# Sixteen-head attention on Trainium2: score matmuls on 32 rows of the array, over dense q and k stacks

## What is computed

```python
scores = einsum('bthd,bshd->bhts', q, k) / sqrt(8)
scores = where(causal, scores, -inf)      # third of the three stages only
attn = softmax(scores, axis=-1)
out = einsum('bhts,bshd->bthd', attn, v)
x = x + out @ Wo + bo                     # first and third stage; the second has no projection
```

## Time and profile before

| | us |
|---|---|
| median of 3 runs | 2067.69 (2063.5 to 2068.28) |
| profiled execution | 2068.89 |
| its span in the profile | 2066.9 |
| PE busy over the span | 1612.5 (78%) |
| DVE busy | 1384.6 (67%) |
| ACT busy | 944.4 (46%) |
| POOL busy | 776.1 (38%) |

### The profile page before, as it was taken

The page is one execution under the profiler, slowest core; times in us unless marked ns, Lnnn a source line. Parts: engine busy times, 40 slices in busy tenths (PEclk is TensorE's granted clock), DMA queues, the critical chain, the costliest instruction groups (busy, mean ns, idle before and its releaser), DMA issues. The chain is left out here.

```text
span 2066.9 us, 42332 instructions
## 1 busy us (share of the span) xinstructions
PE 1612.5 (78%) x14686; PEld 1273.3 (62%) x14686; DVE 1384.6 (67%) x4103; ACT 944.4 (46%) x1817; POOL 776.1 (38%) x1156
## 2 busy tenths in 40 slices
PE   5888873877799989788885899998549799999440
PEld 3666552876577778455553566665449699997330
DVE  4777754238787777577775799997547577774632
ACT  2666630533343334366663677777114344443010
POOL 2222226345300000211113677774454544442435
PEclk9999985887799999699997899999559799999555
DMA  6131301841000000000000000000038000000043
GB/s 181 49 129 69 107 6 37 251 143 41 25 1 2 0 1 1 6 9 7 8 5 1 1 2 2 2 2 1 16 113 234 22 15 13 14 14 3 21 135 89
DMA packets 60417, 91.88 MB, mean 44 GB/s; under 512 B 11588, under 2 KB 49493, under 8 KB 59669
## 3 DMA queue, kind: packets, MB, share of 16 engines
q1 hardware_dynamic: 54068, 76.67, 12.1%
q0 software_dynamic: 6144, 12.60, 2.1%
HBM read 72.71 MB, written 35.39 MB: 52 GB/s over the span
## 5 line engine op out<-in xcount | busy, mean ns | idle before, releaser
L666 DVE TENSOR_REDUCE parts<-PS 128x8 fp32r<-128x1024 f32 x192 | 234.8, 1223 | 120.5 <-PE PS L424 119.4
L862 ACT ACTIVATE P<-PS 128x1024 f32<-128x1024 f32 x192 | 197.0, 1026 | 153.6 <-PE PS L439 153.4
L840 ACT CAST qS<-PS 32x512 fp32r<-32x512 f32 x384 | 220.9, 575 | 9.1 <-PE PS L391 5.7
L272 POOL TENSOR_TENSOR ve<-mv,eps_t 128x1 f32<-128x1 f32 x160 | 33.1, 207 | 443.1 <-DVE mv L268 443.0
L1633 DVE SCALAR_TENSOR_TENSOR X<-PS,wt,X 128x128 f32 (+1 forms) x480 | 134.7, 344 | 47.3 <-PE PS L1476 39.7
L1476 PEld LDWEIGHTS PS<-w_f_w,P 128*128 128x128 f32 x1024 | 130.0, 193 | 39.2 <-issue 27.3
L1765 ACT ACTIVATE P<-PS,w_f_b 128x512 f32<-128x512 f32 x128 | 88.0, 687 | 142.2 <-PE PS L1457 140.8
L1476 PE MATMUL PS<-w_f_w,P 128*128 128x128 f32 x1024 | 142.1, 283 | 13.1 <-DVE X L1633 11.2
L439 PE MATMUL PS<-qS,kS 128*128 128x512 f32 x384 | 148.0, 440 | 1.0 <-ACT P L862 1.0
L760 POOL TENSOR_TENSOR rrs<-rsq,neg_half 128x20 f32<-128x20 f32 x32 | 114.3, 3571 | 74.2 <-DVE rsq L595 74.2
L391 PE MATMUL PS<-ident_r,parts 128*128 128x128 f32 x768 | 122.1, 292 | 23.2 <-issue 22.5
(11 more groups left out here) (300 smaller groups left out, 4283.4 us busy)
## 6 DMA issues: line engine op xcount, KB each, us to landing
tok<-hs SPq DMA_DIRECT2D x62, 128.0 KB, 3.2
hs<-yo SPq DMA_DIRECT2D x62, 128.0 KB, 3.6
P<-in_f_blob SPq DMA_DIRECT2D x12, 578.0 KB, 4.7
Y<-in_f_blob SPq DMA_DIRECT2D x11, 578.0 KB, 4.9
ctxT<-in_ctxT SPq DMA_DIRECT2D x128, 48.0 KB, 1.7
P<-in_f_blob SPq DMA_DIRECT2D x12, 450.0 KB, 4.0
Y<-in_f_blob SPq DMA_DIRECT2D x11, 450.0 KB, 4.2
w_f_w<-in_f_w SPq DMA_DIRECT2D x2, 1024.0 KB, 5.7
```

What stands on the lines that cost most here:

```text
L666: e.tensor_reduce(parts[:, it.s, 0, 8 * half:8 * half + 8, 3, 0], S_ps[:, :, :].rearrange("p i (j t) -> p (i j) t", t=T), AXX, ALU.max)\
L840: m = e.copy(qS[r, it.s % 2, :, j, :], TP[0][r, :].rearrange("p (g t) -> p g t", g=4))
L862: e.activation(P[:, it.s % 2, 8 * half:8 * half + 8, :].rearrange("p h t -> p (h t)"), ST_ps[:, :, :].rearrange("p j n -> p (j n)"), ACT.E ...
```

## The change

In the three stages the maximum is now taken from the same split stacks as the probabilities. `pe_turn`, `v_kx`/`a_kx`, `a_qT` and the block-diagonal `a_qS` are gone. `pe_stack_q` and `pe_stack_k` run at lag L, before the maximum is known; ACT copies them whole (`a_qA`, `a_kS`). `pe_scores` then makes one matmul per head: 24 array rows of `qA` (the parts without the maximum's place) against 24 rows of `kD`, 128 columns, eight matmuls a half that go in turn to two blocks of 32 array rows. When the maxima are in `parts`, `pe_stack_q_max` (lag L + 1) turns the q stack a second time and `a_qB` copies it; `pe_scoresT` (lag L + 1) makes one matmul per head on 32 rows, again eight a half. L becomes 3 or 5, while the last lag O stays 6 or 9. The three tiles `qA`, `qB`, `kD` lie in the memory of the old `qS`. The order of the steps on PE and ACT is written anew, one order for all three stages. In the masked stage POOL clears `vx` at the start; in the cross stage its clearing of `qS` is gone. The parameter `pre` is given by no caller, so `lead` is 0 and its branches are not built.

```diff
-            L = 4 if causal else 2
-            G = L + 4
-            O = L + 5 if causal else L + 4
+            L = 5 if causal else 3
+            G = L + 3
+            O = L + 4 if causal else L + 3
...
-            n_pad = 3 if kind == "cross" else 2 if masked else 0
-            s_turn, s_kx, s_qT = sem("turn"), sem("kx"), sem("qT")
-            s_tk, s_kS, s_tq, s_qS = (sem(n) for n in ("tk", "kS", "tq", "qS"))
+            n_pad = 3 if masked else 2 if kind == "cross" else 0
...
+            stacks = qS[:].rearrange("p b g j t -> p (b g j t)")
+            qA = stacks[:, 0:1024].rearrange("p (b g t) -> p b g t", b=2, g=4)
+            qB = stacks[:, 1024:2048].rearrange("p (b g t) -> p b g t", b=2, g=4)
+            kD = stacks[:, 2048:4096].rearrange("p (b g t) -> p b g t", b=RING, g=4)
...
-                before_it = it.n - (L - F) + 1
-                if due(before_it):
-                    e.wait_ge(s_kx, at(s_kx, before_it))
-                    e.wait_ge(s_qT, at(s_qT, before_it))
+                if due(it.n):
+                    e.wait_ge(s_fr, at(s_fr, it.n))
...
-            def pe_turn(e, it):
-
-                e.wait_ge(s_fr, at(s_fr, following(it, L - F)))
-                e.wait_ge(s_qkf, at(s_qkf, (2 if causal else 1) * (it.n + 1)))
-                for which in range(2):
-                    m = e.transpose(FR[:, which * T:(which + 1) * T],
-                                    qk[:, it.s % 2, which, :, :].rearrange("p h d -> p (h d)"), ident[:, :])
-                m.then_inc(s_turn, 1)
...
             def pe_stack_k(e, it):
                 e.wait_ge(s_lo, at(s_lo, 2 * it.n + 2))
-                if due(it.n - (O - L - 1)):
-                    e.wait_ge(s_added, at(s_added, it.n - (O - L - 1)))
-                if causal and due(it.n - (G - L - 1)):
-                    e.wait_ge(s_eg, at(s_eg, it.n - (G - L - 1)))
+                if due(it.n - (O - L)):
+                    e.wait_ge(s_added, at(s_added, it.n - (O - L)))
+                if causal and due(it.n - (G - L)):
+                    e.wait_ge(s_eg, at(s_eg, it.n - (G - L)))
                 if due(it.n):
                     e.wait_ge(s_kS, at(s_kS, it.n))
-                turn_stack(e, it, 1, s_tk)
+                turn_stack(e, it, 1, 1, s_tk)
 
             def pe_stack_q(e, it):
                 e.wait_ge(s_lo, at(s_lo, 2 * it.n + 2))
+                if due(it.n - 1):
+                    e.wait_ge(s_qB, at(s_qB, it.n - 1))
+                turn_stack(e, it, 0, 0, s_t1)
+
+            def pe_stack_q_max(e, it):
                 e.wait_ge(s_mx, at(s_mx, 2 * it.n + 2))
-                if due(it.n):
-                    e.wait_ge(s_qS, at(s_qS, it.n))
-                turn_stack(e, it, 0, s_tq)
+                e.wait_ge(s_qA, at(s_qA, following(it, 2)))
+                turn_stack(e, it, 0, 0, s_t2)
 
             def pe_scores(e, it, half):
                 if half == 0:
-                    e.wait_ge(s_qT, at(s_qT, it.n + 1))
-                    e.wait_ge(s_kx, at(s_kx, it.n + 1))
+                    e.wait_ge(s_kS, at(s_kS, it.n + 1))
+                    e.wait_ge(s_qA, at(s_qA, it.n + 1))
                 if due(2 * it.n + half):
                     e.wait_ge(s_mx, at(s_mx, 2 * it.n + half))
                 if causal:
                     for i in range(2):
                         e.matmul(S_ps[:, i, :], ident_r[:, :], causal_q[:, :], start=True, stop=False)
-                for i in range(2):
-                    r = 32 * (2 * half + i)
-                    m = e.matmul(S_ps[:, i, :], qT[r:r + 32, it.s, :],
-                                 kx[r:r + 32, it.s % 2, :, :].rearrange("p j t -> p (j t)"),
-                                 start=not causal, stop=True)
+                for g in range(4):
+                    for i in range(2):
+                        r = 32 * (2 * half + i)
+                        m = e.matmul(S_ps[:, i, g * T:(g + 1) * T], qA[r:r + 24, it.s % 2, g, :],
+                                     kD[r:r + 24, it.s, g, :], start=not causal, stop=not causal or g == 3)
                 m.then_inc(s_s, 1)
...
             def pe_scoresT(e, it, half):
                 if half == 0:
-                    e.wait_ge(s_kS, at(s_kS, it.n + 1))
-                    e.wait_ge(s_qS, at(s_qS, it.n + 1))
+                    e.wait_ge(s_qB, at(s_qB, it.n + 1))
                 if due(2 * it.n + half):
                     e.wait_ge(s_exp, at(s_exp, 2 * it.n + half))
-                for i in range(2):
-                    g = 2 * half + i
-                    if causal:
+                if causal:
+                    for i in range(2):
                         e.matmul(ST_ps[:, i, :], ident_r[:, :], causal_k[:, :], start=True, stop=False)
-                    m = e.matmul(ST_ps[:, i, :], kS[:, it.s % 2, g, :],
-                                 qS[:, it.s % 2, g, :, :].rearrange("p j t -> p (j t)"),
-                                 start=not causal, stop=True)
+                for g in range(4):
+                    for i in range(2):
+                        r = 32 * (2 * half + i)
+                        m = e.matmul(ST_ps[:, i, g * T:(g + 1) * T], kD[r:r + 32, it.s, g, :],
+                                     qB[r:r + 32, it.s % 2, g, :], start=not causal, stop=not causal or g == 3)
                 m.then_inc(s_st, 1)
...
-                                     P[:, it.s % 2, 4 * g + j, :], start=(j == 0), stop=(j == 3))
+                                     P[:, it.s % 2, 4 * j + g, :], start=(j == 0), stop=(j == 3))
...
+                for item in unrolled(O + lead):
+                    if it := item(L + lead):
+                        pe_stack_q(e, it)
+                        pe_stack_k(e, it)
+                    if it := item(L + 2 + lead):
+                        pe_values(e, it, 0)
+                    if it := item(L + 1 + lead):
+                        pe_stack_q_max(e, it)
+                    if it := item(L + lead):
+                        pe_scores(e, it, 0)
+                    if it := item(L + 2 + lead):
+                        pe_values(e, it, 1)
+                    if it := item(L + 1 + lead):
+                        pe_scoresT(e, it, 0)
+                    if it := item(F + lead):
+                        pe_hT(e, it)
+                    if it := item(L + lead):
+                        pe_scores(e, it, 1)
+                    if causal and (it := item(G)):
+                        pe_gate(e, it)
+                    if it := item(L + 1 + lead):
+                        pe_scoresT(e, it, 1)
+                    if it := item(F + lead):
+                        pe_qkv(e, it)
+                    if it := item(O + lead):
+                        pe_out(e, it)
...
-            def v_kx(e, it):
-                e.wait_ge(s_turn, at(s_turn, it.n + 1))
-                e.tensor_tensor(kx[:, it.s % 2, :, :], FR[:, T:2 * T].unsqueeze(1).broadcast_to([D, 4, T]),
-                                jmask[:, :].unsqueeze(2).broadcast_to([D, 4, T]), ALU.mult).then_inc(s_kx, 1)
...
-                e.tensor_reduce(parts[:, it.s, 0, 8 * half:8 * half + 8, 3, 0],
-                                S_ps[:, :, :].rearrange("p i (j t) -> p (i j) t", t=T), AXX, ALU.max)\
+                e.tensor_reduce(parts[:, it.s, 0, :, 3, 0].rearrange("p (g j) -> p j g", j=4)[:, 2 * half:2 * half + 2],
+                                S_ps[:, :, :].rearrange("p i (g t) -> p i g t", t=T), AXX, ALU.max)\
                  .then_inc(s_mx, 1)
...
+                if masked:
+                    e.memset(vx[:], 0.0).then_inc(s_pad, 1)
                 if kind == "cross":
-                    e.memset(qS[:].bitcast(F32), 0.0).then_inc(s_pad, 1)
...
             def a_kS(e, it):
+                if due(2 * (it.n - RING + 1)):
+                    e.wait_ge(s_st, at(s_st, 2 * (it.n - RING + 1)))
+                e.wait_ge(s_tk, at(s_tk, it.n + 1))
+                e.copy(kD[:, it.s].rearrange("p g t -> p (g t)"), TP[1]).then_inc(s_kS, 1)
+
+            def a_qA(e, it):
+                if due(2 * (it.n - 1)):
+                    e.wait_ge(s_s, at(s_s, 2 * (it.n - 1)))
+                e.wait_ge(s_t1, at(s_t1, it.n + 1))
+                e.copy(qA[:, it.s % 2].rearrange("p g t -> p (g t)"), TP[0]).then_inc(s_qA, 1)
+
+            def a_qB(e, it):
                 if due(2 * (it.n - 1)):
                     e.wait_ge(s_st, at(s_st, 2 * (it.n - 1)))
-                e.wait_ge(s_tk, at(s_tk, it.n + 1))
-                e.copy(kS[:, it.s % 2].rearrange("p g t -> p (g t)"), TP[1]).then_inc(s_kS, 1)
-
-            def a_qS(e, it):
-                if due(2 * (it.n - 1)):
-                    e.wait_ge(s_st, at(s_st, 2 * (it.n - 1)))
-                e.wait_ge(s_tq, at(s_tq, it.n + 1))
-                for j in range(4):
-                    r = slice(32 * j, 32 * j + 32)
-                    m = e.copy(qS[r, it.s % 2, :, j, :], TP[0][r, :].rearrange("p (g t) -> p g t", g=4))
-                m.then_inc(s_qS, 1)
...
```

(14 more changed lines are left out.)

190 lines of the change are left out of this document (53 added, 137 removed).

## The result

The changed kernel took 2542.96 us (median of 4 runs, 2526.4 to 2556.19), the kernel before 2067.53: a ratio of 1.230, 95% interval 1.227 to 1.233. It is slower, as predicted, but by 475 us and not by 90, far outside the range of 2085 to 2235. The profiled execution took 2526.4 us with a span of 2524.6.

What follows compares the result with a forecast made beforehand. It took a chain over several engines, closed by ACT, to bound the cross stage, and full DVE the self stage. 2068.9 + 47 + 9 + 2 + 32 = 2158.9, median 2158 us; range 2085 to 2235.

Steps and rivals of the forecast that it cites:

- The clock: Self stage: PE idling about 2.0 per tick drops its clock; 16 of 27 ticks at 2 each, +32, bounds 0 and 81.
- Groups of eight: PE's eight score matmuls per half run as four rounds of two, 0.64 a group; bounds 0.50 and 1.08.
- The estimate of 0.84: Length of a PE score group if a block cannot load its next head while working; noted, but 0.64 was kept.
- The wait of the k stack: Self stage: PE stands still about 2.0 per tick before the k stack, until DVE's residual ends.
- The no-wait rival: The residual is in time and PE does not wait at the k stack; faster, about 2052, chance 0.10.
- The self tick: Self stage, steady clock: the chain through PE and DVE lengthens the tick from 9.70 to 11.45.
- the +47: Self stage: cost of the k stack's wait for the residual, 1.75 per tick over 27 ticks.
- The cross tick: Cross stage: a new chain through PE takes what ACT gives back; tick 8.08 against 7.92.
- Clearing `vx`: Start of the masked stage: every engine waits for POOL to clear 2176 columns, +1.9.
- ACT's busy time: Sign in the changed profile: falls by at least 168, from 288 fewer copies of 0.585.
- DVE's share in the self stage: Sign in the changed profile: DVE's busy share falls from 95.7% to about 80%.
- the cross ring: Cross and masked stages: the new chain through PE costs 0.16 per tick, 28 ticks in each, +9.

Runs made afterwards that it cites:

- e5_burst: Changed kernel plus one burst of 24 overwritten 128-row, 512-column matmuls in the 13th sequence of the cross and masked stages; 2533.28 us (1.225).
- e3_residual_first: Changed kernel with DVE adding the residual ahead of the rotation in the self stage; 2365.2 us (1.148).
- e1_all_rows: Changed kernel plus two overwritten 128-row, 512-column matmuls ahead of each half of the maximum's scores, cross and masked stages; median 2500.25 us (1.183 from two executions).
- e4: Kernel before with only the transposed scores made dense, one matmul per head, and one q-stack copy in place of four; 2157.6 us (1.043).
- e2_32_rows: Changed kernel plus two overwritten 32-row, 512-column matmuls ahead of each half of the maximum's scores, cross and masked stages; 2577.97 us (1.243).
- e9: Kernel before with dense transposed scores, one overwritten all-row matmul ahead of each transposed half, hT copied ahead of the first exponential (cross, masked stages); 2114.01 us (1.022).
- e7: Kernel before with dense transposed scores and two overwritten all-row 512-column matmuls ahead of each transposed half, cross and masked stages; 2087.34 us (1.010).
- e6: Changed kernel with its dense maximum kept but transposed scores put back to four block-diagonal copies and 512-column matmuls; 2362.38 us (1.141).

## Why the prediction was wrong

The direction was right, and so were the durations and waits at the upper level. The step that failed is **The clock**: it was sized at +32 with bounds 0 and 81, for the self stage alone, and took some 400: about 115 in the self stage and 286 in the two others, (297 less 9 and 2, below), where the prediction had it at nothing.

- **Groups of eight.** 0.64 predicted, 0.66 measured at the upper level (L423 at 184.18 in e5_burst). The estimate of 0.84 that came from the Trainium skill, "TensorE: Matmul & The Clock Gate", Part 3, is not borne out: the eight loads on two row groups cost no more than the sum from the rows.
- **The wait of the k stack.** About 2.0 predicted, 2.08 and 2.09 measured, 47.1 in all in 25 stacks. e3_residual_first removed it by moving the residual alone, which shows the cause. The no-wait rival falls.
- **The self tick.** 11.45 predicted with a steady clock. The tick from 1749.26 to 1762.47 is 13.21; its values, stack and causal pair at the lower level took 0.68, 0.46 and 0.48 more than at the upper one (1.08, 0.66, 0.68 in e1_all_rows and e3_residual_first). Without them it is 11.6. DVE's first maximum waits 3.16 in it (1754.22), with the same three taken off 1.54, where 1.5 was predicted. So the +47 was about right, and of the +162 in this stage some 115 is the clock, where I had 32. The mechanism was right, its size wrong: 16 ticks with 2 each. In a stretch like 1600 to 1700 the level is low for most of the time, so that nearly everything takes double, not the values alone. I had taken the one example of the earlier trace rows, in which PE recovered soon, for the cost of every fall.
- **The cross tick.** 8.08 predicted, 8.15 in the tick of e5_burst that ran at the upper level. But in the changed kernel the stage ran at the lower level: 12.85. The difference, 4.70, by 28 to 32 ticks in each of two stages is 263 to 301; the two stages together lost 297. For this part the prediction had nothing: "In the cross stage PE idles 1.0 a tick with the clock granted at 1.00". That row was read as a property of the stage, and it was one of the work: each tick had four matmuls of 128 rows by 512 columns, which the change takes out. In the kernel before, cross stage, they are these, 1.45 of 7.92:

```profile
132.24 0.73 PE L439 MATMUL PS<-qS,kS 128*128 128x512 f32 x2
...
135.51 0.72 PE L439 MATMUL PS<-qS,kS 128*128 128x512 f32 x2
```

  The level hung on them in part: without them alone it is 0.76 (e4), and e1_all_rows against e2_32_rows, and e9 and e7, show it rising as such work is added. But e6, which keeps them, is at 0.76 too, so it hung on the rest of the mix as well.
- **What would have shown it.** Nothing in the trace of before shows the cross loop without its long all-row matmuls, so the level of the new loop was unknown there, and should have been bounded from both sides like any other price that no row shows: from 0 to doubling every row of PE. The row for the upper end was at hand, the 1.93 of the earlier trace rows against 1.08. The predicted tick of 8.08 holds some 7.3 of PE's work (8.08 less the waits of 0.41 and 0.33 above); by 1.93 / 1.08 that is 13.1, 5.0 more in each of 56 ticks, 280. With it and the self stage's own bound of 81 the slow end would have been about 2490, near the 2543, and not 2235.
- **The other terms.** Clearing `vx` took 1.94 as worked out (1.9). ACT's busy time fell by 151 (944.4 to 793.4) and not by 168. Its instructions taken one by one fell as worked out: 282.9 went (L840 220.9, L821 36.5, L826 25.5) and 112.5 came (L797, L803), 170 less; busy time counts overlapping instructions once, and the kernel before had more overlap. DVE's share in the self stage fell to 53 and 62% instead of 80%, since the tick is longer than predicted.

By terms, against 458 between the spans: 47 for the wait in the self stage, 9 for the cross ring, 2 for the clearing, and what is left, 400, for the clock. The first three were in the sum.

The Trainium skill, "TensorE: Matmul & The Clock Gate", Part 1, says that the gate opens by how busy PE has been, so that sustained work runs at the upper level and long idle stretches lose it. The self stage agrees in the direction (2.08 idle and a fall; no wait for the residual and 1.00). The masked stage doesn't: 98.78 of 100 us busy, 0.19 idle in the tick from 1195.37, and 0.50. The measurement decides; by that rule alone the changed loop would have run at 8.15.

**Open.** What about the long all-row matmuls counts, their rows, their length together with the rows, or their operands, was not separated beyond 128 rows against 32 at the same columns, where the pairs also ran one after the other or at once. Nor was it tested what the second q stack alone, or the dense maximum alone, does to the level. Why e1_all_rows mostly held the level in the cross stage and mostly lost it in the masked one, and why two of its four executions took over 100 more than the others, isn't settled either.

## What to carry to other kernels

Replacing wide matmuls, zeros and all, by exact small ones on part of the array's rows can cost the clock: here block-diagonal matmuls that are three quarters zeros kept PE at 2.4 GHz, and the dense ones left it 99% busy at 1.2 GHz. When a change takes the long all-row matmuls out of a loop, price every PE row at both levels and let the range hold both. A step moved forward on an in-order engine takes its wait along: look at what the wait is for (here a residual at the end of DVE's tick), and move that first; and in a ring, look for a short step queued behind a long one on the engine that closes it, as hT was behind the exponential.

## What the runs showed of the hardware

- A granted clock at its lower level with TensorE busy for 98 to 100 of 100 us, for hundreds of microseconds, in the changed kernel and in e2_32_rows (0.50 from 1000 to 1300 in both) and in e5_burst (0.50 from 1200 to 1300, 98.65 busy).
- The same number of matmuls and columns gave 1.00 with the added ones on 128 rows and 0.50 with them on 32 (e1_all_rows and e2_32_rows, 200 to 300).
- Long all-row matmuls in the tick don't secure the level: 0.76 in e6_dense_max_only with four of them, 0.50 in the masked stage of e1_all_rows with four (1200 to 1300).
- 24 long all-row matmuls (8.04 us) lifted the level, and it fell again within about 11 us of their end, under a loop without long idle stretches (e5_burst, 184.18 to 195.32).
- Added work can shorten a loop: 12.85 per tick in the changed kernel, 8.66 with four more matmuls in each (e1_all_rows, cross stage).
- The profile's clock column can show 1.00 in an early stretch where the durations are those of the lower level (changed kernel, 100 to 200: 1.00 beside values of 1.94).
